# Inverse square roots in a decoder layer: a tuned seed, one tuned Newton step and one step of third order

## The chip, the cores and the metric

The kernel runs on one core of a Trainium2 chip. The metric is the device time of one execution in microseconds (us). The engines are TensorE (PE in the profile), VectorE (DVE), ScalarE (ACT), GpSimd (POOL) and SyncE (SP); they run side by side and wait for each other on semaphores.

## The reference

Input x is 8 sequences of 256 tokens with 256 features. One decoder layer is applied, in float32:

```
x = x + mamba(layernorm(x))            # in-projection, 4-tap convolution, chunked state scan, gated RMS norm, out-projection
x = x + cross(layernorm(x), context)   # 16 heads of 64, with an additive mask
x = x + ffn(layernorm(x))              # causal attention, 16 heads of 16, and 4 experts, top 2, both behind an RMS norm
# layernorm: (x - mean) / sqrt(var + 1e-5);  RMS norm: x * rsqrt(mean(x*x) + eps) * gain
```

Every norm needs one inverse square root for each token. A token is a row, so a group of 512 tokens has 4 values in each of the 128 partitions.

## The kernel before

The weights are loaded once and split into a high and a low part, so that three products of rounded operands give one product of float32 precision (`split_matmul`, L97 to L102, whose operations all carry the lines L100 to L102). Then four groups of 512 tokens go one after the other through three stages: `stage_mamba` (tiles a_), `stage_cross` (b_) and `stage_attention` (c_). Each stage is a block: all engines meet at its end. At the end `stage_experts` (e_) routes all 2048 tokens and runs 35 tiles of 128 slots through the experts. The order of the work on each engine is the order in which the code is written; nothing is scheduled by a program.

`inverse_root_of` takes values in one tile of a pair, uses the other as scratch, and writes their inverse square roots. `inverse_root` first adds the epsilon. All operations are on DVE and have 2 to 8 elements in each partition. `Chain.link` issues an operation and makes DVE wait until it has finished, `Chain.then` issues it without waiting for it. There are 25 calls:

- one in `load_weights` (through `normed`, tile w_rstd), for the first group,
- in each group one at the end of `stage_mamba` (L629, tile a_rs), in front of the scaling of the out-projection (L633). PE has by then filled two banks with out-projections and waits for L633 before it fills them again,
- one at the start of `stage_cross` (L942, b_rstd), while PE projects the context,
- one at the start of `stage_attention` (L1360, c_roots, 8 elements: two norms at once), which all PE work of the stage follows,
- one for the next group's first norm (L1424, through `normed`, c_rstn), while PE and ACT lay out the attention's operands,
- two at the end of `stage_attention` (L1454, c_rs, 2 elements each), one for each half of the group, in front of L1456.

Of the kernel before, what the change touches and what calls it, by code (L numbers as in the profile page):

```python
# [7 lines left out]
I32 = mybir.dt.int32  # L8
FR = mybir.dt.float32r
ALU = mybir.AluOpType  # L10
# [121 lines left out]
def inverse_root(dve, ch, out, var, eps, tmp):  # L132

    ch.link(dve.tensor_scalar(tmp[1], var, eps, None, ALU.add))
    inverse_root_of(dve, ch, out, tmp)


def inverse_root_of(dve, ch, out, tmp):

    hv, t = tmp  # L140
    ch.then(dve.tensor_scalar(hv, t, -0.5, None, ALU.mult))
    ch.link(dve.tensor_scalar(out.bitcast(I32), t.bitcast(I32), 1, None, ALU.logical_shift_right))
    ch.link(dve.tensor_scalar(out.bitcast(I32), out.bitcast(I32), -1.0, float(0x5F3759DF), ALU.mult, ALU.add))
    for _ in range(3):
        ch.link(dve.tensor_tensor(t, out, out, ALU.mult))
        ch.link(dve.tensor_tensor(t, t, hv, ALU.mult))
        ch.link(dve.scalar_tensor_tensor(out=out, in0=t, scalar=1.5, in1=out, op0=ALU.add, op1=ALU.mult))


def normed(dve, ch, out, x, st, mv, rstd, nt, ready):  # L150
# [892 lines left out]
def stage_attention(nc, ctx, g, I, W, K, XN, XG, RAW, rows_of, ps, s, weights_in, last):  # L1043

    weights, at_rows, at_out = rows_of
    with ExitStack() as own:
# [305 lines left out]
        def _(dve):  # L1352
# [5 lines left out]
            ch.link(dve.scalar_tensor_tensor(out=nt2[:, 1, 1], in0=nt2[:, 1, 0], scalar=RMS_EPS, in1=mv[:, :, 1],  # L1358
                                             op0=ALU.mult, op1=ALU.add))
            inverse_root_of(dve, ch, roots[:], (nt2[:, 0], nt2[:, 1]))  # L1360
            for t in range(GT):
                dve.tensor_scalar(xr[:, t, :], XG[:, t, :], mv[:, t, 0:1], scale[:, t:t + 1],
# [584 lines left out]
```

How the kernel before makes its waits and increments, by code:

```python
    def sync(self):  # L115
        if self.n:
            self.eng.wait_ge(self.sem, self.n)
# [43 lines left out]
def transposes_in(pe, src, ident, banks, tiles, ready, done):  # L161
    for t in range(GT):
        pe.wait_ge(ready, t + 1)
        for k in range(tiles):
            ins = pe.transpose(banks[k][:, t * P:(t + 1) * P], src[:, t, k * P:(k + 1) * P], ident)
            if t == GT - 1:
                ins.then_inc(done, 1)
# [30 lines left out]
        @block.sync  # L199
        def _(sp):
            sp.dma_start(XN[:], I["x"][0]).then_inc(s["x_in"], 16)
            for n, src in raws:
                sp.dma_start(raw[n][:], src).then_inc(loaded[n], 16)
            sp.wait_ge(s["x_in"], 16)
            sp.sem_inc(stored, 32)
# [1 line left out]
        @block.tensor  # L207
        def _(pe):
            pe.wait_ge(s["const_in"], 16)
            transposes_in(pe, xn, K["const"][:, C_ID:C_ID + P], ps, KD, s["x_normed"], s["x_turned"])
# [1 line left out]
        @block.scalar  # L212
        def _(act):
            act.dma_start(K["const"][:], I["const"][:, 0:C_N]).then_inc(s["const_in"], 16)
            for n in ("rope", "taps", "tapb", "nw", "g1", "g2", "dtb", "alog", "dpar"):
                act.dma_start(K[n][:], I[n]).then_inc(s["small_in"], 16)
            for i, (n, _) in enumerate(raws):
                if n == "wout":
                    act.wait_ge(s["wout_scaled"], 1)
                act.wait_ge(loaded[n], 16)
                act.activation(W[n][0][:], raw[n][:], ACT.Copy).then_inc(s["high_parts"], 1)
                if i == 1:
```

## Time and profile before

| | us |
|---|---|
| runs, median of 3 | 1502.42 (1502.37 to 1502.48) |
| profiled execution | 1502.61 |
| its span in the trace | 1500.7 |
| PE busy | 1225.5 (82%), 7994 matmuls |
| DVE busy | 1008.9 (67%), 3074 instructions |
| ACT busy | 638.3 (43%) |
| POOL busy | 265.4 (18%) |
| DMA, 16 engines | 80.32 MB, 54 GB/s |
| mean granted clock of TensorE | 0.90 of full speed |

The span is cut into engines' busy times. The clock of TensorE has two levels in this trace, 1.00 (2.4 GHz) and 0.50 (1.2 GHz); a stretch's mean between the two says that it held some of both. A wait of an engine that is not on the path to the end costs nothing, so the busy shares say where work is, not what a shorter operation is worth. For that one reads at each place who waits for whom.

### The profile page before, as it was taken

The numbers are of one execution on the slowest core, as the hardware profiler recorded it, in microseconds if no ns is written. First come the engines' busy times: TensorE is split into PE (matmuls) and PEld (weight loads), VectorE is DVE, ScalarE is ACT, GpSimd is POOL, SyncE is SP. The second block draws the span as 40 slices with busy tenths as digits, with TensorE's granted clock in tenths as the row PEclk, the third lists the DMA queues.
The fourth block names the chain that finished last, engine by engine and source line by source line (L and its number), as shares of the span: only waits on it lengthen the run. The fifth ranks groups of instructions, "written<-read, shape, count | busy, mean of one in ns | idle before, by whom it ended". The sixth has DMA issues, their size and how long they took to land. (4 is left out here: it accounts for less than half of the span.)

```text
span 1500.7 us, 24288 instructions
## 1 busy us (share of the span) xinstructions
PE 1225.5 (82%) x7994; PEld 1086.0 (72%) x7994; DVE 1008.9 (67%) x3074; ACT 638.3 (43%) x1370; POOL 265.4 (18%) x199
## 2 busy tenths in 40 slices
PE   1679987968799697779996968799787149999997
PEld 1467986946689696567996946689687148888886
DVE  6875766668477666785766668567667875555553
ACT  4325635733266175324644723256265403333331
POOL 2200003311000150100003301000141612333332
PEclk9889997988899888789997987899889559999999
DMA  6005510010164001004510010064330001222221
GB/s 231 1 1 123 136 38 1 2 56 1 42 145 96 15 1 42 15 1 113 134 36 15 1 57 1 22 154 106 143 125 10 21 14 25 40 36 36 37 41 23
DMA packets 45256, 80.32 MB, mean 54 GB/s; under 512 B 8432, under 2 KB 18160, under 8 KB 44496
## 3 DMA queue, kind: packets, MB, share of 16 engines
q1 hardware_dynamic: 36976, 69.19, 17.1%
q0 software_dynamic: 6720, 9.18, 3.8%
q8 instruction: 69, 1.13, 0.3%
q10 hardware_dynamic: 1440, 0.39, 0.1%
q14 instruction: 51, 0.42, 0.1%
HBM read 28.01 MB, written 8.78 MB: 25 GB/s over the span
## 5 line engine op out<-in xcount | busy, mean ns | idle before, releaser
L921 ACT ACTIVATE b_pp<-b_pp,b_nm 128x256 f32<-128x256 f32 x256 | 116.0, 501 | 86.9 <-DVE b_nm L959 86.0
L800 PEld LDWEIGHTS bank<-b_va,b_pt 128*128 128x128 f32 x1024 | 127.6, 191 | 4.0
L800 PE MATMUL bank<-b_va,b_pt 128*128 128x65 f32 x1024 | 128.5, 269 | 0.0
L1187 PE MATMUL bank<-c_kv,c_qv 128*128 128x128 f32 (+1 forms) x512 | 95.5, 316 | 7.3 <-ACT c_kv L1302 7.3
L1209 PE MATMUL bank<-c_v,c_pt 128*128 128x68 f32 x768 | 101.1, 268 | 0.1
L1145 POOL TENSOR_SCALAR c_qv<-c_rot,const 128x512 fp32r<-128x512 f32 x56 | 86.8, 1567 | 77.9 <-ACT c_rot L1298 77.9
L1209 PEld LDWEIGHTS bank<-c_v,c_pt 128*128 128x128 f32 x768 | 97.9, 192 | 1.7 <-DVE c_pt L1409 0.7
L959 DVE CUSTOM_DVE_ANT_0 b_pp<-bank,mask 128x256 f32<-128x256 f32 x256 | 97.0, 418 | 0.0
L100 PE MATMUL bank<-e_up_low,e_xh 128*128 x210 | 89.7, 427 | 1.8 <-DVE e_xl L178 1.8
L1401 DVE CUSTOM_DVE_ANT_0 c_pp<-bank,const 128x128 f32<-128x128 f32 (+1 forms) x256 | 80.2, 351 | 10.0 <-PE bank L1187 10.0
L1568 POOL DMA_INDIRECT out<-e_ys,e_ids x35 | 55.5, 1586 | 164.2 <-DVE e_ys L1803 160.4
L102 PE MATMUL bank<-e_up_high,e_xh 128*128 x210 | 84.3, 401 | 0.0
L1128 POOL MEMSET c_v<- 128x16 f32 x4 | 0.5, 126 | 473.0 <-POOLq L643 473.0
L787 PE MATMUL bank<-const,b_pp 128*128 128x128 f32 x512 | 77.7, 274 | 7.8 <-ACT b_pp L921 7.7
L101 PE MATMUL bank<-e_up_high,e_xl 128*128 x210 | 83.6, 398 | 0.0
L1672 ACT ACTIVATE e_th<-bank 128x512 f32<-128x512 f32 x35 | 21.0, 601 | 146.5 <-PE bank L102 146.5
L1786 DVE SCALAR_TENSOR_TENSOR e_th<-e_th,bank 128x512 f32<-128x512 f32 x70 | 38.8, 554 | 65.7 <-ACT e_th L1672 57.1
L773 PE MATMUL bank<-k_low_twice,b_qst 128*128 128x256 f32 x256 | 76.0, 321 | 7.1 <-DMA b_qst<-b_ql 7.1
L1187 PEld LDWEIGHTS bank<-c_kv,c_qv 128*128 128x128 f32 x512 | 73.3, 209 | 10.2 <-ACT c_kv L1302 10.2
L178 DVE SCALAR_TENSOR_TENSOR b_ql<-bank,b_qst 64x512 fp32r<-64x512 f32 x64 | 44.0, 688 | 52.4 <-ACT b_qst L892 30.9
L515 DVE SCALAR_TENSOR_TENSOR a_cv<-bank,taps,a_cv 128x510 f32<-128x510 f32 (+2 forms) x72 | 53.7, 746 | 37.3 <-ACT a_cv L461 35.6
L332 POOL TENSOR_TENSOR a_av<-a_a,const 128x1024 f32<-128x1024 f32 x16 | 30.2, 1896 | 244.5 <-DVE a_a L549 159.8
(368 smaller groups left out, 3631.2 us busy)
## 6 DMA issues: line engine op xcount, KB each, us to landing
b_kst<-b_kh SPq DMA_DIRECT2D x128, 128.0 KB, 2.3
k_low_twice<-b_kl SPq DMA_DIRECT2D x128, 128.0 KB, 2.4
b_qst<-b_ql SPq DMA_DIRECT2D x64, 128.0 KB, 2.3
raw_up<-in_w SPq DMA_DIRECT2D x4, 768.0 KB, 10.3
raw_down<-in_w SPq DMA_DIRECT2D x4, 768.0 KB, 12.1
XN<-in_x SPq DMA_DIRECT2D x5, 512.0 KB, 3.4
context<-in_ctxT SPq DMA_DIRECT2D x4, 512.0 KB, 4.7
mask<-in_mask SPq DMA_DIRECT2D x4, 512.0 KB, 5.6
```

What stands on the lines that cost most here:

```text
L100: pe.matmul(out, ah, bl, start=start, stop=False)
L101: pe.matmul(out, al, bh, start=False, stop=False)
L102: return pe.matmul(out, ah, bh, start=False, stop=stop)
L773: pe.matmul(out, qst[:, j % 2, hp, tokens(b, qt)], klst[j % 2][:, hp, b * S:(b + 1) * S], start=True, stop=False)
L787: ins = pe.transpose(T2[n % 2][:, kt * S + qt * P:kt * S + (qt + 1) * P], pp[:, n % 3, qt, kt * P:(kt + 1) * P], ident)
L800: ins = pe.matmul(O2[u % 2][:, at:at + VW], pt[:, n % 2, kt * S + qt * P:kt * S + (qt + 1) * P], va[:, b * QT + kt, 2 * j + hp, :], start= ...
L921: act.activation(pp[:, n % 3, qt, :], pp[:, n % 3, qt, :], ACT.Exp, bias=nm[:, n % 4, qt:qt + 1], scale=-1.0).then_inc(s["probs_exp"], 1)
L959: dve.tensor_tensor_reduce(out=pp[:, n % 3, qt, :], in0=S3[n % 3][:, qt * S:(qt + 1) * S], in1=mask[:, b * QT + qt, :], scale=-1.0, scalar ...
L1145: pool.tensor_scalar(qv[:, m % 2, r, :], qb, rows(r), None, ALU.mult).then_inc(s["q_masked"], 1)
L1187: ins = pe.matmul(SB[n % 3][:, qt * P:qt * P + w], qv[:, m % 2, r, at:at + P], kv[:, m % 2, part, b * S:b * S + w], start=part == 0, stop= ...
L1209: ins = pe.matmul(OB[u % 2][:, at:at + AKV * AVW], pt[:, n % 4, i * P:(i + 1) * P], v[:, b * QT + kt].rearrange("p a b -> p (a b)"), start ...
L1401: dve.tensor_tensor_reduce(out=pp[:, n % 4, w], in0=SB[n % 3][:, w], in1=causal[:, (QT - 1 - qt) * P:QT * P], scale=-AD ** -0.5, scalar=3e ...
```

## The change

`inverse_root_of` is rewritten. Before: an operation that scales the input, an integer shift and an integer subtraction for the seed, and three Newton steps of three operations, twelve in all. After: the seed in one operation (the value's bits times -0.5 plus a constant), a Newton step of three operations with tuned constants and a sign that is put right later, and a step of third order in five operations, of which one (the scaling of `out`) is issued without waiting for it: nine in all. Each call has three DVE operations fewer, 75 over the kernel. Nothing else in the code differs.

```
 def inverse_root_of(dve, ch, out, tmp):
-    hv, t = tmp
-    ch.then(dve.tensor_scalar(hv, t, -0.5, None, ALU.mult))
-    ch.link(dve.tensor_scalar(out.bitcast(I32), t.bitcast(I32), 1, None, ALU.logical_shift_right))
-    ch.link(dve.tensor_scalar(out.bitcast(I32), out.bitcast(I32), -1.0, float(0x5F3759DF), ALU.mult, ALU.add))
-    for _ in range(3):
-        ch.link(dve.tensor_tensor(t, out, out, ALU.mult))
-        ch.link(dve.tensor_tensor(t, t, hv, ALU.mult))
-        ch.link(dve.scalar_tensor_tensor(out=out, in0=t, scalar=1.5, in1=out, op0=ALU.add, op1=ALU.mult))
+    q, x = tmp
+    ch.link(dve.tensor_scalar(out.bitcast(I32), x.bitcast(I32), -0.5, float(0x5F1FFFF9), ALU.mult, ALU.add))
+    ch.link(dve.tensor_tensor(q, out, out, ALU.mult))
+    ch.link(dve.tensor_tensor(q, q, x, ALU.mult))
+    ch.link(dve.scalar_tensor_tensor(out=out, in0=q, scalar=-ROOT_A, in1=out, op0=ALU.add, op1=ALU.mult))
+    ch.link(dve.tensor_tensor(q, out, out, ALU.mult))
+    ch.then(dve.tensor_scalar(out, out, -0.375 * ROOT_B ** 5, None, ALU.mult))
+    ch.link(dve.tensor_tensor(q, q, x, ALU.mult))
+    ch.link(dve.scalar_tensor_tensor(out=q, in0=q, scalar=-10 / (3 * ROOT_B ** 2), in1=q, op0=ALU.add, op1=ALU.mult))
+    ch.link(dve.scalar_tensor_tensor(out=out, in0=q, scalar=5 / ROOT_B ** 4, in1=out, op0=ALU.add, op1=ALU.mult))
```

with `ROOT_B = 0.703952253` and `ROOT_A = 2.38924456`. Six lines are added above, so lines behind L147 are numbered 6 higher in the changed kernel.

This is DVE's order at the end of the mamba stage before (a_nt is the pair of scratch tiles, a_rs the result, L633 the scaled out-projection):

```order
L134 TENSOR_SCALAR a_nt<-a_ss 128x4
L141 TENSOR_SCALAR a_nt<-a_nt 128x4
L142 TENSOR_SCALAR a_rs<-a_nt 128x4
L143 TENSOR_SCALAR a_rs<-a_rs 128x4
L145 TENSOR_TENSOR a_nt<-a_rs 128x4
L146 TENSOR_TENSOR a_nt<-a_nt 128x4
L147 SCALAR_TENSOR_TENSOR a_rs<-a_nt,a_rs 128x4
...
L633 SCALAR_TENSOR_TENSOR XG<-bank,a_rs,XN 128x256
```

The three lines from L145 stand three times there. The same place in the changed kernel:

```order
L134 TENSOR_SCALAR a_nt<-a_ss 128x4
L145 TENSOR_SCALAR a_rs<-a_nt 128x4
L146 TENSOR_TENSOR a_nt<-a_rs 128x4
L147 TENSOR_TENSOR a_nt<-a_nt 128x4
L148 SCALAR_TENSOR_TENSOR a_rs<-a_nt,a_rs 128x4
L149 TENSOR_TENSOR a_nt<-a_rs 128x4
L150 TENSOR_SCALAR a_rs<-a_rs 128x4
L151 TENSOR_TENSOR a_nt<-a_nt 128x4
L152 SCALAR_TENSOR_TENSOR a_nt<-a_nt 128x4
L153 SCALAR_TENSOR_TENSOR a_rs<-a_nt,a_rs 128x4
L639 SCALAR_TENSOR_TENSOR XG<-bank,a_rs,XN 128x256
```

Between the epsilon and the scaling stand nine operations where twelve stood. No operation of another engine moves.

## Rows read from the trace of the kernel before

**Rows 1.** Timeline of DVE at the first group's mamba norm: start us, us, engine, line

```profile
94.53 0.17 DVE L141 TENSOR_SCALAR a_nt<-a_nt 128x4 f32<-128x4 f32 x1
94.61 0.16 DVE L142 TENSOR_SCALAR a_rs<-a_nt 128x4 int32<-128x4 int32 x1
...
96.78 0.48 DVE L633 SCALAR_TENSOR_TENSOR XG<-bank,a_rs,XN 128x256 f32<-128x256 f32 x1
```

**Rows 2.** Timeline of DVE at the attention stage's first norm and its last but one

```profile
222.78 0.17 DVE L141 TENSOR_SCALAR c_nt<-c_nt 128x8 f32<-128x8 f32 x1
...
225.07 1.38 DVE L1362 TENSOR_SCALAR c_xr<-XG,moments,c_roots 128x256 f32<-128x256 f32 x4
...
302.72 0.17 DVE L141 TENSOR_SCALAR c_nt<-c_nt 128x2 f32<-128x2 f32 x1
...
304.95 0.62 DVE L1456 TENSOR_SCALAR c_xr<-c_ln,c_rs 128x256 f32<-128x256 f32 x2
```

**Rows 3.** Timeline of PE behind these norms: in brackets idle before, and its releaser

```profile
97.41 0.55 PE L100 MATMUL bank<-wout_low,a_yh 128*128 128x256 f32 x1 [2.94 <-DVE XG L633]
...
225.54 0.69 PE L166 MATMUL bank<-const,c_xr 128*128 128x128 f32 x2 [5.55 <-DVE c_xr L1362]
...
305.63 0.55 PE L1220 MATMUL bank<-const,c_xr 128*128 128x128 f32 x3 [1.28 <-DVE c_xr L1456]
```

**Rows 4.** Timeline of DVE behind the load's and the cross stage's norm

```profile
18.26 4.46 DVE L260 TENSOR_TENSOR wv_low<-raw_wv,wv_high 128x2048 fp32r<-128x2048 f32 x1 [0.87 <-ACT wv_high L221]
...
111.16 0.69 DVE L950 COPY b_va<-bank 128x512 f32<-128x512 f32 x1 [1.55 <-PE bank L102]
```

**Rows 5.** Stretches: length, busy us of PE, PEld, DVE, ACT, POOL, then PEclk

```profile
107.30:110.60 3.30, 3.30 (x9) 2.56 (x8) 2.13 (x9) 0.60 (x1) 0.00 (x0) 0.50 0.00 0
315.50:318.88 3.38, 3.38 (x10) 2.17 (x9) 0.00 (x0) 0.67 (x2) 0.00 (x0) 0.50 0.94 326
318.88:322.30 3.42, 3.42 (x17) 2.66 (x17) 2.55 (x6) 1.82 (x3) 0.00 (x0) 1.00 0.04 16
336.00:342.70 6.70, 5.71 (x30) 5.07 (x30) 4.78 (x8) 3.64 (x7) 0.00 (x0) 0.75 0.00 0
598.80:602.19 3.39, 3.39 (x11) 2.24 (x10) 0.00 (x0) 0.98 (x2) 0.00 (x0) 0.50 0.88 324
602.19:605.60 3.41, 3.41 (x16) 2.71 (x16) 2.85 (x7) 1.81 (x4) 0.00 (x0) 1.00 0.00 0
1237.10:1243.80 6.70, 6.33 (x22) 4.66 (x21) 2.64 (x6) 1.50 (x4) 0.00 (x0) 0.75 0.00 0
```

**Rows 6.** Timeline of PE where its work begins again in three of these stretches

```profile
313.48 0.58 PE L100 MATMUL bank<-ul,win_high 128*8 128x512 f32 x1 [2.11 <-PEq L1046]
...
336.13 0.80 PE L100 MATMUL bank<-ul,win_high 128*128 128x512 f32 x1 [2.35 <-DVE a_cv L515]
...
1235.17 0.79 PE L100 MATMUL bank<-e_up_low,e_xh 128*128 x1 [1.45 <-DVE e_xl L178]
```

**Rows 7.** Timeline, two places of the mamba stage in the second and the third group

```profile
347.63 1.19 PE L401 MATMUL bank<-a_av,const 128*128 128x512 f32 x1 [0.71 <-DVE a_zg L564]
...
376.77 0.17 DVE L134 TENSOR_SCALAR a_nt<-a_ss 128x4 f32<-128x4 f32 x1
...
630.62 1.19 PE L401 MATMUL bank<-a_av,const 128*128 128x512 f32 x1 [0.71 <-DVE a_zg L564]
...
659.91 0.17 DVE L134 TENSOR_SCALAR a_nt<-a_ss 128x4 f32<-128x4 f32 x1
```

**Rows 8.** Timeline of DVE, two places of the attention stage in both groups

```profile
530.17 0.29 DVE L1401 CUSTOM_DVE_ANT_0 c_pp<-bank,const 128x128 f32<-128x128 f32 x1 [2.04 <-PE bank L1187]
...
583.13 0.42 DVE L1444 TENSOR_TENSOR c_ln<-c_ln,bank 128x256 f32<-128x256 f32 x1 [0.32 <-PE bank L102]
...
813.01 0.29 DVE L1401 CUSTOM_DVE_ANT_0 c_pp<-bank,const 128x128 f32<-128x128 f32 x1 [1.98 <-PE bank L1187]
...
866.19 0.42 DVE L1444 TENSOR_TENSOR c_ln<-c_ln,bank 128x256 f32<-128x256 f32 x1 [0.32 <-PE bank L102]
```

More of the change, by code:

```diff
@@ L135, in inverse_root @@
     inverse_root_of(dve, ch, out, tmp)
+ROOT_B = 0.703952253
+ROOT_A = 2.38924456
 def inverse_root_of(dve, ch, out, tmp):
-    hv, t = tmp
-    ch.then(dve.tensor_scalar(hv, t, -0.5, None, ALU.mult))
-    ch.link(dve.tensor_scalar(out.bitcast(I32), t.bitcast(I32), 1, None, ALU.logical_shift_right))
-    ch.link(dve.tensor_scalar(out.bitcast(I32), out.bitcast(I32), -1.0, float(0x5F3759DF), ALU.mult, ALU.add))
-    for _ in range(3):
-        ch.link(dve.tensor_tensor(t, out, out, ALU.mult))
-        ch.link(dve.tensor_tensor(t, t, hv, ALU.mult))
-        ch.link(dve.scalar_tensor_tensor(out=out, in0=t, scalar=1.5, in1=out, op0=ALU.add, op1=ALU.mult))
+    q, x = tmp
[8 more added lines that the diff above has]
+    ch.link(dve.scalar_tensor_tensor(out=out, in0=q, scalar=5 / ROOT_B ** 4, in1=out, op0=ALU.add, op1=ALU.mult))
 def normed(dve, ch, out, x, st, mv, rstd, nt, ready):
```

## The prediction

> **What bounds the kernel now.** I read the busy shares first: PE 82%, DVE 67%, so neither is the bound throughout, and a shorter DVE chain is worth something only where others wait for it. Next the timeline at each of the seven kinds of call, one by one, asking who starts right behind the chain; last the granted clock by stretches, because the page's row of clock digits is under 9 in some slices, and these slices repeat from group to group.
>
> At three kinds of place the chain is what everybody waits for. Behind the mamba norm PE has been idle 2.94 us when L633 lets it go on; behind the attention stage's first norm 5.55 us; behind the first of its two last norms 1.28 us [rows 3]. The second of the last two follows the first through DVE's own order (add, square, norm), and the stage's end follows it. At the other three kinds nobody waits. In the load, the wv split that DVE comes to later waits 0.87 us for ACT, which waits for weights. In the cross stage DVE has its norm done and then idles 1.55 us for PE [rows 4]. The next group's norm ends in an idle DVE too: 2.04 us until the scores come [rows 8].
>
> **The change part by part.** The chain before runs from L141 at 94.53 to L633 at 96.78, 2.25 us [rows 1]. L141 isn't waited for and costs 0.08 (94.53 to 94.61); the other eleven operations take 96.78 - 94.61 = 2.17, 0.197 each, start to start. The chain after has eight operations that are waited for and one that is not: 8 x 0.197 + 0.08 = 1.66. Saved: 0.59. With 8 elements the chain is 225.07 - 222.78 = 2.29, with 2 elements 304.95 - 302.72 = 2.23 [rows 2]; the same count gives 0.61 and 0.58. All kinds of operation in the new chain stand in the old one, so I take no other duration. If the unwaited operation cost a full slot, the saving would be 0.47; if it cost nothing, 0.67.
>
> On the path in each group: 0.59 + 0.61 + 2 x 0.58 = 2.36. Over four groups 9.4 us. The thirteen other calls I cost at nothing: four cross norms (cover 1.55), four of the next group (cover 2.04) and the one of the load (cover: ACT and the weights). I don't need their covers for more than 0.59, and they aren't used up: what stands behind them moves earlier by less than the chain. The bound on the load's call is 0 to 0.6. No wait is added, no DMA moves.
>
> **What the clock makes of it.** That 9.4 would be the answer if PE's clock didn't change under way. It does. In the second group the clock is at 0.50 (1.2 GHz) up to 318.88 and at 1.00 (2.4 GHz) behind it; in the third it is at 0.50 up to 602.19 [rows 5]. The two rises are 283.31 apart, although the work itself had by then moved: L401 starts 282.99 after its twin, 0.32 early against the rises, but L134, behind another low stretch in between, 283.14 after, 0.17 early [rows 7]. In the attention stage the same: 282.84, that is 0.47 early, going into the low stretch, and 283.06, 0.25 early, behind it [rows 8]. So the rises sit at times of their own, and where PE is the bound on both sides of one, what arrives d earlier leaves only d/2 earlier: the extra time before the rise is spent at half rate. I apply this half three times in a group: in the mamba stage, at the start of the cross stage (PE is without a gap at 0.50 from 107.30 to 110.60 [rows 5]), and in the attention stage. At the fronts of stages, where DVE is the bound, d passes in full.
>
> Group 1: nothing before the mamba norm. Then 0.59 saved; DVE waits for PE again at the last of the out-projections that follow, and part of them runs at the low clock, so that I keep 0.40 of it (between a half, 0.3, and all, 0.59); half in the cross stage, 0.20; + 0.61 = 0.81; half, 0.40; + 1.16 = 1.56 at the end of the group.
>
> If all rises stayed where they are, that would go on as d/8 + 1.6 and end near 1.8: locked. But they will not all stay. Before the rise at 318.88 PE had been without a gap since 313.48 [rows 6], 5.4 us. Other rises come after less: PE starts at 336.13, and the stretch from 336.00 to 342.70 has a mean of 0.75, so half of it is low and the rise is near 339.35, 3.2 us behind the start. With a start 1.56 earlier, at 311.92, I expect the rise one step earlier, and the low part of 3.35 us just read is that step: 318.88 goes to about 315.5, 3.5 us behind the start. I take the step as 3.4. What PE did at half rate in the 5.4 us is then done in 3.6 us at half rate and the rest, 1.8 us of half-rate work, in 0.9: at 316.4 in place of 318.9, d = 2.5, and DVE's convolutions follow with all of it. Against rises that all come 3.4 early this is 0.9 behind, which the next halving makes 0.5. If this rise didn't move, I expect the later one of the mamba stage to do so, since PE would then reach L401 1.56 earlier and be past its gap of 0.71 [rows 7]; either way the second group leaves its mamba stage 3.4 - 0.5 = 2.9 early. Then + 0.59 = 3.5, excess over a step 0.1; cross 0; + 0.61, halved, 0.3; + 1.16 = 1.5. From there each group repeats itself: one step, with an excess of 1.5 at its end. After four groups: 3 x 3.4 + 1.5 = 11.7.
>
> In the experts the routing before the first tile shifts as a whole. The first tile's projections start at 1235.17 [rows 6] and the clock rises half way through 1237.10 to 1243.80, near 1240.45 [rows 5], 5.3 us later. With an excess of 1.5 it is as in the second group: the rise comes one step sooner against the start. The low part shrinks from 5.3 to 3.4, and half of 1.9, 0.95, is gained. Behind it PE bounds every tile and nothing is lost. Sum: 11.7 + 0.95 = 12.6 (without that last step the excess is halved, and the sum is 10.9).
>
> The profiled execution took 1502.61 and gives 1490.0; it is 0.19 above the median of the runs, so against the median 1489.8. That is my forecast.
>
> The Trainium skill, "TensorE: Matmul & The Clock Gate", section "What's actually happening", says that where the clock rises differs from run to run and that one shouldn't fit to it. By that rule the steps average out and the gain is the plain 9.4. The times here speak against it: three runs lie within 0.11 us of each other, and a whole step would show.
>
> **The rivals.**
> A. Plain sum: the steps come at other places than I walked, and on average d passes in full. 9.4 saved, 1493.0. For it: my walk hangs on two margins (0.4 at the second group's rise, 0.2 at the experts'). Against: the halvings are measured.
> B. Locked: no rise moves. 1.8 at the end of the groups, halved in the experts: 0.9 to 1.8 saved, 1500.6 to 1501.5. For it: the groups repeat at 283.31 as if nothing else could be. Against: 1.56 is much more than the 0.3 that the groups drifted.
> C. Slower: the earlier arrival puts idle time together so that the clock falls once more in PE's gapless work. The place would be the start of the scores in the attention stage, where PE starts and stops. A low stretch of 3.4 costs 1.7, one of 10.2 (three steps) 5.1. It decides from two extra long ones in each group: 8 x 1.7 = 13.6 against 9.4, 4.2 slower, 1506.6. Against: PE's idle times get shorter with this change, not longer (2.94, 5.55 and 1.28 all shrink).
> D. The change doesn't do what it says: DVE's operations with a multiply and an add on integers, or the chain's last steps, cost a slot more each, and 0.2 and not 0.59 is saved: plain sum 3.2, 1499.2.
>
> **How the numbers follow.** Forecast with the experts' step 0.42, without it (10.9 saved, 1491.5) 0.2, A 0.2, B 0.06, C 0.02, D 0.04; 0.06 for more than forecast, a further step of 3.4 somewhere (cost 1.7), 1488.1. The range takes in the forecast, the case without the step, A with its 0.47 for a chain (7.5 saved would be 1494.9, a corner of A) in part, and the further step: 1488.0 to 1493.8. About 0.2% (3.0 us) is what a measurement of this kernel can tell from no change. Faster by more than that: all but B, C and half of D, 0.91; within: 0.07; slower: 0.02.
>
> **What would show it.** Each chain 1.65 to 1.70 long in place of 2.25. L633's waiter on PE idle about 2.4. The rises at the start of the groups no longer 283.31 apart but one step less, about 279.9, and the groups with them; the first group still ending only about 1.56 early. The experts' first rise 3.4 behind their first projection. If the groups are 281 apart with rises at uneven distances, A is right; if the rises stay at 283.31, B. I would be wrong altogether if the attention stage showed a low stretch that it hasn't now.

## The result: 12.1 us faster

| | before | changed |
|---|---|---|
| runs, median | 1502.45 us (1502.09 to 1504.98, 6 runs) | 1490.33 us (1489.40 to 1491.48, 6 runs) |
| ratio, 95% interval | | 0.9915 (0.9902 to 0.9928) |
| profiled execution | 1502.61 us | 1490.08 us |
| its span | 1500.7 us | 1488.2 us |
| DVE busy | 1008.9 us, 3074 instructions | 995.1 us, 2999 instructions |
| PE busy | 1225.5 us | 1221.8 us |

The forecast was 1489.8. The 12.1 us are 0.8% of the time. Sixteen chains on the path lose about 0.6 us each, 9.4 us in sum. Where the other 2.7 us come from is the subject of what follows.

The chain itself first. DVE's timeline at the first group's mamba norm in the changed kernel (start us, duration us, engine, line); it answers to [rows 1]:

```profile
94.67 0.17 DVE L145 TENSOR_SCALAR a_rs<-a_nt 128x4 int32<-128x4 int32 x1
94.88 0.16 DVE L146 TENSOR_TENSOR a_nt<-a_rs 128x4 f32<-128x4 f32 x1
...
95.66 0.17 DVE L150 TENSOR_SCALAR a_rs<-a_rs 128x4 f32<-128x4 f32 x1
95.74 0.15 DVE L151 TENSOR_TENSOR a_nt<-a_nt 128x4 f32<-128x4 f32 x1
...
96.32 0.48 DVE L639 SCALAR_TENSOR_TENSOR XG<-bank,a_rs,XN 128x256 f32<-128x256 f32 x1
```

From 94.67 to 96.32 it is 1.65 us, where 2.25 stood. L150 isn't waited for and costs 0.08 (95.66 to 95.74); every other step is about 0.2. With two elements the changed chain takes 304.04 - 302.40 = 1.64, by the first and the last of these rows:

```profile
302.40 0.17 DVE L145 TENSOR_SCALAR c_rs<-c_nt 128x2 int32<-128x2 int32 x1
...
304.04 0.61 DVE L1462 TENSOR_SCALAR c_xr<-c_ln,c_rs 128x256 f32<-128x256 f32 x2
```

PE's idle time behind the three norms, with the first operation after it (in brackets the idle time and who ended it); the rows answer to [rows 3]:

```profile
96.95 0.36 PE L100 MATMUL bank<-wout_low,a_yh 128*128 128x256 f32 x1 [2.33 <-DVE XG L639]
...
224.94 1.33 PE L172 MATMUL bank<-const,c_xr 128*128 128x128 f32 x5 [4.95 <-DVE c_xr L1368]
...
304.71 0.66 PE L1226 MATMUL bank<-const,c_xr 128*128 128x128 f32 x4 [0.67 <-DVE c_xr L1462]
```

2.94, 5.55 and 1.28 have become 2.33, 4.95 and 0.67: 0.61, 0.60 and 0.61 less. In the cross stage, where the chain was held to be hidden, the wait has grown instead. This DVE row answers to the second of [rows 4], which had 1.55:

```profile
111.17 0.69 DVE L956 COPY b_va<-bank 128x512 f32<-128x512 f32 x1 [2.42 <-PE bank L102]
```

Its start has not moved (111.16 before): DVE is done earlier and waits longer for PE. So far this is only the plain sum. The rest is seen where PE's work begins again: at the front of the second, third and fourth group, and at the experts' first tile. PE in the changed kernel:

```profile
311.72 0.59 PE L100 MATMUL bank<-ul,win_high 128*8 128x512 f32 x1 [2.11 <-PEq L1052]
...
591.63 0.58 PE L100 MATMUL bank<-ul,win_high 128*8 128x512 f32 x1 [2.12 <-PEq L1052]
...
871.12 0.58 PE L100 MATMUL bank<-ul,win_high 128*8 128x512 f32 x1 [2.15 <-PEq L1052]
...
1223.43 0.79 PE L100 MATMUL bank<-e_up_low,e_xh 128*128 x1 [1.45 <-DVE e_xl L184]
```

Two of the same places of the kernel before (the other two starts, 313.48 and 1235.17, are in [rows 6]):

```profile
596.48 0.59 PE L100 MATMUL bank<-ul,win_high 128*8 128x512 f32 x1 [2.12 <-PEq L1046]
...
879.54 0.58 PE L100 MATMUL bank<-ul,win_high 128*8 128x512 f32 x1 [2.11 <-PEq L1046]
```

| | before | changed | gained so far | forecast |
|---|---|---|---|---|
| front of group 2 | 313.48 | 311.72 | 1.76 | 1.56 |
| front of group 3 | 596.48 | 591.63 | 4.85 | 1.56 + 3.4 = 4.96 |
| front of group 4 | 879.54 | 871.12 | 8.42 | 8.36 |
| experts' first tile | 1235.17 | 1223.43 | 11.74 | 11.7 |
| span | 1500.7 | 1488.2 | 12.5 | 12.6 |

The gain comes in steps of 3.1, 3.6 and 3.3, more than the 2.36 that the chains of a group give. The granted clock around these fronts (columns: length, busy us of PE, PEld, DVE, ACT, POOL, then the granted clock, the DMA share and GB/s), against [rows 5]:

```profile
309.10:315.80 6.70, 4.59 (x13) 2.38 (x12) 1.91 (x5) 1.43 (x3) 0.00 (x0) 0.50 0.70 223
315.85:322.60 6.75, 6.75 (x31) 4.96 (x31) 5.00 (x10) 2.33 (x4) 0.00 (x0) 1.00 0.23 90
589.00:595.70 6.70, 4.58 (x13) 2.34 (x12) 1.91 (x5) 1.43 (x3) 0.00 (x0) 0.50 0.72 221
595.75:602.50 6.75, 6.75 (x31) 4.96 (x31) 5.00 (x10) 2.33 (x4) 0.00 (x0) 1.00 0.23 89
868.90:875.60 6.70, 4.55 (x12) 2.54 (x12) 1.67 (x5) 1.43 (x3) 0.00 (x0) 0.50 0.75 238
875.65:882.40 6.75, 6.75 (x31) 5.01 (x31) 5.23 (x10) 2.33 (x4) 0.00 (x0) 1.00 0.18 72
1220.00:1227.20 7.20, 4.43 (x11) 3.29 (x12) 0.79 (x3) 1.22 (x3) 2.48 (x3) 0.50 0.25 73
1227.25:1234.00 6.75, 6.37 (x33) 4.92 (x33) 3.91 (x9) 2.33 (x7) 0.00 (x0) 1.00 0.00 0
```

The rise of the clock stands near 315.8, 595.7 and 875.6, that is 279.9 apart where it was 283.3 (318.88 and 602.19 in [rows 5]). From PE's start to the rise PE now spends 4.1, 4.1 and 4.5 us at 0.50 (1.2 GHz), before 5.4, 5.7 and 5.95; in the experts 3.8 in place of 5.3. That is 5.8 us less at half rate, and what is done at full rate instead takes half, so an estimate of the gain is 2.9 us. With the plain sum of 9.4 it makes 12.3, and 12.5 were measured between the two spans. The sum is rough: it takes the 9.4 as passed on in full, while the first group passes on 1.76 of its 2.36, and it leaves out the low stretches further inside the groups.

### The profile page after: what moved, and what is told of

Read it like the earlier page. It is cut to its first block and busy times, and to the rows that moved or that the text cites. A ratio compares the mean times of both kernels' runs of the same rounds, so it can differ in the third digit from the quotient of the medians.

```text
span 1488.2 us, 24213 instructions
## 1 busy us (share of the span) xinstructions
PE 1221.8 (82%) x7994; PEld 1082.5 (73%) x7994; DVE 995.1 (67%) x2999; ACT 639.2 (43%) x1370; POOL 265.3 (18%) x199
## 5 line engine op out<-in xcount | busy, mean ns | idle before, releaser
L1193 PEld LDWEIGHTS bank<-c_kv,c_qv 128*128 128x128 f32 x512 | 73.3, 209 | 10.2 <-ACT c_kv L1308 10.2
L1318 ACT ACTIVATE c_pp<-c_pp,c_nm 128x128 f32<-128x128 f32 x128 | 51.5, 402 | 50.6 <-DVE c_nm L1407 50.5
## 6 DMA issues: line engine op xcount, KB each, us to landing
raw_up<-in_w SPq DMA_DIRECT2D x4, 768.0 KB, 10.1
raw_down<-in_w SPq DMA_DIRECT2D x4, 768.0 KB, 12.1
```

The source lines that it names most:

```text
L1193: ins = pe.matmul(SB[n % 3][:, qt * P:qt * P + w], qv[:, m % 2, r, at:at + P], kv[:, m % 2, part, b * S:b * S + w], start=part == 0, stop= ...
```

## The experiments

Each was measured beside the kernel before, whose median there was 1502.99 (first four below), 1503.82 (next four), 1504.98 and 1504.32 (the last two pairs). Where times of different comparisons are set side by side, these differences of up to 2.5 us have to be kept in mind. Every statement on the clock below comes from one profiled execution of each kernel.

| kernel | median, us | ratio to before, 95% interval |
|---|---|---|
| nine operations at c_rs only | 1492.77 (1492.08 to 1494.64) | 0.9932 (0.9918 to 0.9945) |
| nine at a_rs and c_roots only | 1497.27 (1496.10 to 1500.11) | 0.9963 (0.9949 to 0.9977) |
| ten everywhere | 1491.22 (1490.10 to 1492.73) | 0.9918 (0.9905 to 0.9932) |
| eleven everywhere | 1497.12 (1495.70 to 1498.39) | 0.9956 (0.9943 to 0.9970) |
| nine at the calls on the path | 1489.93 (1489.00 to 1491.10) | 0.9913 (0.9900 to 0.9926) |
| nine at the hidden calls | 1503.61 (1502.11 to 1506.14) | 1.0002 (0.9994 to 1.0011) |
| fifteen everywhere | 1507.64 (1505.63 to 1510.36) | 1.0027 (1.0015 to 1.0039) |
| changed, GpSimd's copy later | 1497.83 (1492.65 to 1498.84) | 0.9957 (0.9944 to 0.9971) |
| PE's waits filled, nine | 1451.56 (1450.18 to 1452.82) | 0.9647 (0.9634 to 0.9660) |
| PE's waits filled, twelve | 1463.33 (1461.15 to 1463.62) | 0.9719 (0.9706 to 0.9733) |
| filled further, nine | 1446.71 (1445.34 to 1456.77) | 0.9634 (0.9607 to 0.9661) |
| filled further, twelve | 1456.66 (1453.10 to 1461.96) | 0.9686 (0.9666 to 0.9706) |

### Which calls bring it: on the path, and hidden

The old function was kept beside the new one as `inverse_root_twelve`, and a call takes one or the other. In the first kernel the load's norm, the cross norm and the next group's norm have the old one; in the second the four calls of each group that are on the path have it instead.

```
-def inverse_root(dve, ch, out, var, eps, tmp):
+def inverse_root(dve, ch, out, var, eps, tmp, root=None):
     ch.link(dve.tensor_scalar(tmp[1], var, eps, None, ALU.add))
-    inverse_root_of(dve, ch, out, tmp)
+    (root or inverse_root_of)(dve, ch, out, tmp)
...
-            inverse_root(dve, ch, rstd[:], mv[:, :, 1], LN_EPS, (nt[:, 0], nt[:, 1]))
+            inverse_root(dve, ch, rstd[:], mv[:, :, 1], LN_EPS, (nt[:, 0], nt[:, 1]), inverse_root_twelve)
```

> Nine operations at the four calls of each group that the prediction puts on the path (mamba norm, attention's first norm, its two last norms), twelve at the load's, the cross stage's and the next group's norm. If those thirteen calls are hidden: the same as the changed kernel, 1490.3. If they count in part (0.59 each, 7.7 in all): up to 1498.

> The complement: nine operations at the load's, the cross stage's and the next group's norm (9 calls), twelve at the others. Hidden: 1502.9, as before. If they count: down to 1495.

Measured: 1489.93 with the calls on the path (the changed kernel has 1490.33), 1503.61 with the hidden ones (before: 1503.82, ratio 1.0002). The sixteen calls on the path bring everything; the other nine (the load's, four cross norms, four of the next group) bring nothing that can be measured. The prediction and the first expectation call them thirteen; the list has nine. No number of the prediction rests on it, but the 7.7 of the expectation does: nine calls of 0.59 are 5.3, and the upper end would have been 1495.6.

### How much of it: ten, eleven and fifteen operations

One, two or three dependent operations that multiply by one were put behind the chain in all 25 calls, in the changed kernel for ten and eleven, in the kernel before for fifteen.

```
     ch.link(dve.scalar_tensor_tensor(out=out, in0=q, scalar=5 / ROOT_B ** 4, in1=out, op0=ALU.add, op1=ALU.mult))
+    for _ in range(1):          # 2 in the second, 3 behind the twelve in the third
+        ch.link(dve.tensor_scalar(out, out, 1.0, None, ALU.mult))
```

> The changed kernel with one more dependent operation of 0.197 us in each chain (a multiplication by 1.0), ten in all: 1.58 of path saved in each group instead of 2.36. Steps: 1.03 is left at the end of the first group, at the edge of what moves the rise at the front of the second group; so either about 1491.3 (it moves) or about 1501.3 (it doesn't), nothing between. Plain sum: 6.3 saved, 1496.1.

> The changed kernel with two more dependent operations of 0.197 us in each chain, eleven in all: 0.8 of path saved in each group. Steps: 0.5 is left at the end of the first group, no rise moves, 0.3 to 0.6 saved in all, 1502.0, groups 283.3 apart. Plain sum: 3.2 saved, 1499.2.

> The kernel before with three more dependent operations (multiplications by 1.0) in each chain, fifteen in all: 2.36 us of path added in each group, as much as the change takes away. Steps: before, the groups are held at 283.31 by the clock's rises, and a later start by 0.6 at the mamba norm, 0.6 and 1.2 in the attention stage leaves (0.3 + 0.6) / 2 + 1.2 = 1.6 to 1.9 of delay that is not added up from group to group; 1.5 to 2.5 slower in all, 1505, groups still 283.3 apart. Plain sum: 9.4 slower, 1512.3, groups 285.6 apart.

Measured: 1490.3, 1491.2, 1497.1, 1502.5 and 1507.6 us with nine, ten, eleven, twelve and fifteen. By the plain sum each operation is worth 16 x 0.197 = 3.15 us. The steps are 0.9, 5.9 and 5.4, and three more cost 3.8 (against its own comparison's 1503.82) to 5.1 (against 1502.5), under the plain 9.4. Against the kernel before of each comparison, nine, ten and eleven save 12.1, 11.8 and 5.9. So the gain isn't proportional, and the steps are where I had put them only in part: of ten I had said that it either stays near nine (1491.3) or falls back to 1501.3, and it stayed. Eleven was expected to fall back to twelve, and came out between nine and twelve, nearer to its plain sum (1499.2) than to that. Fifteen was expected at 1505, with groups 283.3 apart. They are 283.3 apart, but the first group alone costs 5.7 in place of the 1.6 to 1.9 expected: PE begins the second group at 319.19, before at 313.48.

The clock shows why. With eleven operations the rise came 2.91, 5.98 and 3.06 us behind PE's start at the three fronts: in the second and fourth group it came a step earlier, in the third it did not. I had taken it that a rise comes no sooner than 3.2 us after PE's start.

### Which of the calls on the path

> The nine-operation chain stands only at the attention stage's two last norms (8 calls, 1.16 us of path in each group); all other calls have the twelve-operation chain. Steps (the gain is given out in steps of the clock's rises): the second group's matmuls begin 1.16 earlier, which I take to be enough for the rise at its front to come one step of 3.4 earlier in each of three groups; 3 x 3.4 + 1.0 = 11.2 saved, about 1491.2, groups 279.9 apart. Plain sum: 4 x 1.16 = 4.6 saved, 1497.8, groups about 282. The chains that nobody waits for are what counted: 1502.4.

> The nine-operation chain stands only at the mamba norm and at the attention stage's first norm (8 calls, 0.59 + 0.61 = 1.20 us of path in each group, as much as the two last norms have); all others have twelve. Steps: (0.40 / 2 + 0.61) / 2 = 0.4 is left at the end of the first group, too little for a rise to move; about 0.5 saved at the end of the groups and half of it behind the experts' rise, 1502.0, groups 283.3 apart. Plain sum: 4.8 saved, 1497.6, groups about 282.

The edit is the one above, with the new function at c_rs only (8 calls) and at a_rs and c_roots only (8 calls). Measured: 1492.77 and 1497.27. Half of the calls gives 10.2 us, of 12.1 in all, though their plain sum is 4.6; the other half, with a plain sum of 4.8, gives 5.7. Together 15.9, more than both at once: neither has a value of its own. The first result was expected and came 1.6 later than said. The second was not: by the steps no gain had been expected (1502.0). Its plain sum had said 1497.6, which is the time measured, with groups about 282 apart. They are 283.3 and 279.9 apart, so the mean is about that of the plain sum, but it is made up of whole steps. Its stretches around the fronts (columns as above):

```profile
309.10:315.80 6.70, 3.88 (x11) 1.93 (x12) 2.95 (x9) 0.84 (x3) 0.00 (x0) 0.50 0.55 168
315.90:322.50 6.60, 6.60 (x31) 4.93 (x30) 4.20 (x9) 2.81 (x5) 0.00 (x0) 1.00 0.38 140
589.00:595.70 6.70, 3.66 (x11) 1.71 (x12) 3.12 (x10) 0.84 (x2) 0.00 (x0) 0.50 0.52 158
595.80:599.10 3.30, 3.30 (x12) 2.23 (x11) 0.00 (x0) 1.21 (x2) 0.00 (x0) 0.50 0.83 306
599.20:602.50 3.30, 3.30 (x15) 2.67 (x15) 3.08 (x7) 1.60 (x4) 0.00 (x0) 1.00 0.00 0
872.30:879.00 6.70, 3.90 (x11) 1.95 (x12) 2.94 (x8) 0.87 (x3) 0.00 (x0) 0.50 0.54 164
879.10:885.80 6.70, 6.70 (x31) 5.04 (x30) 4.30 (x9) 2.79 (x5) 0.00 (x0) 1.00 0.39 144
```

and PE's starts in it:

```profile
313.04 0.58 PE L100 MATMUL bank<-ul,win_high 128*8 128x512 f32 x1 [2.11 <-PEq L1064]
...
593.16 0.59 PE L100 MATMUL bank<-ul,win_high 128*8 128x512 f32 x1 [2.12 <-PEq L1064]
...
876.22 0.59 PE L100 MATMUL bank<-ul,win_high 128*8 128x512 f32 x1 [2.11 <-PEq L1064]
```

The first front's start at 313.04 is only 0.44 earlier than before (313.48), and the rise is at 315.9, 2.8 us behind it, in place of 318.9. At the next front PE starts at 593.16 and the rise is at 599.2, 6.0 behind it; at the third 2.8 again. The 0.44 understates how much earlier PE comes to the rise, since the clock itself lies otherwise from one execution to the next: its first low stretch begins at 49.62 here and at 49.22 before. Counted from there PE's start is 0.84 earlier. The kernels side by side. The first column of times goes from PE's start at a front to the rise behind it, the second from the last front's rise to PE's start, the third from rise to rise:

| | start to rise, us, fronts of groups 2, 3, 4 | rise to start, us, groups 3, 4 | rise to rise, us | median, us |
|---|---|---|---|---|
| fifteen | 4.64, 4.05, 4.06 | 279.26, 279.24 | 283.3, 283.3 | 1507.6 |
| hidden calls only | 5.69, 5.50, 5.86 | 277.81, 277.44 | 283.3, 283.3 | 1503.6 |
| before | 5.40, 5.70, 5.95 | 277.60, 277.36 | 283.3, 283.3 | 1502.5 |
| a_rs and c_roots | 2.82, 6.00, 2.84 | 277.30, 277.06 | 283.3, 279.9 | 1497.3 |
| eleven | 2.91, 5.98, 3.06 | 277.33, 276.83 | 283.3, 279.9 | 1497.1 |
| c_rs only | 3.29, 3.44, 3.43 | 276.45, 276.46 | 279.9, 279.9 | 1492.8 |
| ten | 3.57, 3.23, 3.51 | 276.66, 276.38 | 279.9, 279.9 | 1491.2 |
| on the path | 4.30, 4.04, 4.06 | 275.86, 275.83 | 279.9, 279.9 | 1489.9 |
| changed | 4.1, 4.1, 4.5 | 275.8, 275.4 | 279.9, 279.9 | 1490.3 |

A rise is early where it stands 279.9 behind the one before, and not where the distance is 283.3. For the first front the distance is taken from the start of the first low stretch: 269.7 in the kernel before and with the hidden calls, 273.1 with fifteen operations, a step later, and 266.2, a step earlier, in the six others. So the early rises number none, two or three, and they sort the medians: 1502 to 1504, 1497, and 1490 to 1493; fifteen, with one rise a step late, has 1507.6. The distance from start to rise alone doesn't tell: fifteen has it as short as the fastest kernels.

The column from rise to start shows how close the kernel before stood to the next step. Fronts that PE began 277.06 us or less behind the last rise got theirs at 279.9, those that it began 277.30 or more behind at 283.3; before had 277.60 and 277.36. The walk had the three early rises of the changed kernel and none before, but its margin was wrong.

### The low stretch in the attention stage

The rival that ended slower had its place at the start of the scores. To get at it, GpSimd's copy of the repeated identity, which the kernel starts at the stage's front, was made to wait for the first norm.

```
             pool.memset(v[:, :, :, AD], 1.0).then_inc(s["ones_set"], 1)
+            pool.wait_ge(s["layer_norm_ready"], GT)
             pool.tensor_copy(repeat[:], identr.bitcast(F32).rearrange("p (a d) -> p a d", d=AD).unsqueeze(2)
```

> The changed kernel with GpSimd's fill of the repeat table (L1135, 1.05 us) put behind the stage's layer norm, where before it held up a DVE operation at the stage's start by 0.7 us (0.88 in place of 0.16). 0.7 us of path saved in each group, 2.8 by the plain sum, 1487.5. Steps: halved behind the attention stage's rise, 0.35 in each group and not added up; 0.3 to 0.6 faster, about 1489.9.

Measured: 1497.83, 7.5 us later than the changed kernel, where 1489.9 was expected; one of its six runs took 1492.65. Stretches at the scores' start, first of this kernel:

```profile
239.20:246.00 6.80, 2.45 (x10) 1.57 (x10) 4.94 (x23) 3.88 (x8) 2.11 (x4) 0.50 0.00 0
246.00:262.90 16.90, 16.89 (x78) 16.70 (x79) 5.91 (x33) 8.21 (x19) 8.39 (x6) 0.50 0.00 0
263.10:270.00 6.90, 6.90 (x66) 6.90 (x64) 4.29 (x23) 4.85 (x13) 1.00 (x1) 1.00 0.01 2
```

then of the changed kernel:

```profile
240.80:251.00 10.20, 7.73 (x36) 7.04 (x36) 4.98 (x26) 6.67 (x14) 4.39 (x3) 0.50 0.00 1
251.10:258.00 6.90, 6.90 (x61) 6.81 (x61) 4.25 (x26) 5.25 (x12) 4.82 (x4) 1.00 0.00 0
```

The low stretch of 10.2 us has become one of 23.9 (239.1 to 263.0), and again in the third group (802.3 to 826.2); in the second and fourth it is 13.6. PE was busy, as the profile models it, for 16.89 of the 16.90 us behind 246.00 and the clock stayed at 0.50 all through them. The rival's mechanism exists; the change didn't set it off, since the kernel before has a low stretch of the same length there, from about 240.3 to 250.6 by the means of these rows:

```profile
239.10:249.30 10.20, 5.98 (x27) 5.11 (x27) 7.15 (x37) 5.50 (x12) 4.19 (x5) 0.56 0.00 1
249.40:256.00 6.60, 6.60 (x55) 6.51 (x53) 3.09 (x16) 5.15 (x13) 5.47 (x4) 0.91 0.00 0
```

(5.7 of 10.2 us is 1.2 at 1.00 and 9.0 at 0.50; 0.91 of 6.6 leaves 1.2 at 0.50.) Why the clock stayed low through those 16.9 us stays open: the waits in front of it differ from the changed kernel's, and no run here varied them one at a time. The early rise at the three fronts (2.81, 4.53 and 2.98 us behind PE's start) was there in this kernel too; its loss is the attention stage's: the fronts of groups 2 and 4, behind the two long stretches, come 6.5 and 10.1 us later than in the changed kernel, the one between them 4.7.

### Taking the low clock out

If the extra 2.7 us are the clock's, the two kernels should be a plain sum apart once the clock doesn't fall. PE's waits were filled with matmuls that write a bank nobody reads at that time, 127 in a group, in the changed kernel and in the kernel before alike. The excerpt has notes in its comments that the code doesn't have.

```
+def fill(pe, bank, W, n):
+    w = W["awo"][0]
+    for _ in range(n):
+        pe.matmul(bank[:], w[:, 0, 0:P], w[:].rearrange("p k n -> p (k n)"), start=True, stop=True)
...
+            fill(pe, O2[0], W, 8)        # ahead of the cross stage's first wait
...
+            fill(pe, OB[0], W, 14)       # the attention stage's front, then 6, and 18 before the scores
...
+                fill(pe, BB, W, (4, 14)[hf])   # in front of c_rs's consumers
```

The others: in the mamba stage 11 and 8 in the convolution, 12 before the scan (behind a wait for the decay rates that was added there), 9 and 6 behind the out-projection's second and last tile; 4 at the cross stage's end; in the attention stage 6 before the first scores and 7 at the end.

> The changed kernel with PE's longer waits in each group filled by matmuls of N=512 whose results nobody reads (into banks that are free there), about 110 in a group, each wait filled to nine tenths at most, so that the clock doesn't fall in the groups. If the clock's low stretches are what sets the groups' lengths: the half-rate work in PE-bound places goes (2 us at a group's front, 1 to 2 behind the mamba norm, 2.4 at the cross stage's front, 3 to 5 in the attention stage), 24 to 36 us in all, 1455 to 1466. If they only went with waits that others set: no faster than 1490, or slower by the filling.

> The same filling in the kernel before (twelve operations in a chain). With no low stretches in the groups there are no steps, and the change is worth its plain sum: 9.4 us slower than the filled kernel with nine (8.5 to 10.5), groups 2.36 longer. If the steps aren't from the clock, the difference is 12, as without the filling.

Measured: 1451.56 and 1463.33, 11.8 apart. Both are far faster than their unfilled twins, by 39 us, the first by more than the 24 to 36 expected. But the difference was still 11.8, not 9.4, which by the expectation as written spoke for steps that aren't from the clock, unless the filling had left low stretches. The view of the first GpSimd copy of the attention stage, the same work once in each group, gives the distance from group to group: first and last start, divided by three. Filled with nine, then filled with twelve (count, shortest/median/longest ns, first and last start us):

```profile
L1153 POOL CAST c_repeat<-identr x4: 1037/1054/1057, 218.5 to 1027.5; 128x1024 fp32r<-128x1024 f32 x4
```

```profile
L1147 POOL CAST c_repeat<-identr x4: 1042/1056/1057, 220.3 to 1039.2; 128x1024 fp32r<-128x1024 f32 x4
```

(1027.5 - 218.5) / 3 = 269.7 and 273.0: 3.3 apart, still a step and not 2.36. The filling had left low stretches, and not the same ones. With nine there is one in each group, of 6.8 us (the first one at 64.1 to 71.0; here the second group's):

```profile
333.80:340.60 6.80, 5.90 (x15) 3.25 (x16) 3.79 (x9) 1.24 (x3) 0.50 (x1) 0.50 0.00 0
340.60:603.40 262.80, 246.47 (x1709) 218.33 (x1707) 188.34 (x636) 130.16 (x281) 34.83 (x29) 1.00 0.21 51
```

with twelve one more of 3.4 us in each group's attention stage (239.9, 513.0, 786.0, 1059.1); these two rows have that of the first group and the second group's other one:

```profile
239.90:243.30 3.40, 3.40 (x11) 2.60 (x10) 2.35 (x8) 2.42 (x5) 1.86 (x2) 0.50 0.02 5
338.90:345.70 6.80, 5.22 (x11) 2.68 (x12) 3.79 (x8) 1.29 (x3) 1.45 (x1) 0.50 0.00 0
```

So more was filled: 17 in place of 12 before the scan, 21 in place of 18 before the scores, three before each of two waits of the mamba and attention stages, and 26 before the experts' first tile.

```
-                    fill(pe, SM, W, 12)
+                    fill(pe, SM, W, 17)
...
+            pe.wait_ge(s["weights_high"], 1)
+            fill(pe, UC, W, 26, wh[0][:, 0, 0, 0:512].rearrange("p (k n) -> p k n", k=2))
```

> The filled kernel with nine operations still has one low stretch of 6.8 us in each group (first at 333.8), and its groups are 269.7 apart. Here the waits in front of it, and PE's wait before the first expert's tile, are filled too. No low stretch left between the first group and the routing: 1.5 us less in each group and 2 less in the experts, 1442 to 1447, and the groups free to take any length.

> The same with twelve operations. Steps from the clock: with no low stretch there are no steps, so the change is worth its plain sum: 9.4 us slower than with nine (8.9 to 9.9), every group 2.36 longer. If a low stretch stays in the groups, as in the two kernels filled less, the difference is a whole number of steps again (3.4 in a group, 11.8 measured there). If the steps have another cause: 11 to 12.

Measured: 1446.71 and 1456.66, 9.95 apart, where the plain sum says 9.4. The copies of the two kernels:

```profile
L1154 POOL CAST c_repeat<-identr x4: 1037/1056/1057, 218.7 to 1024.1; 128x1024 fp32r<-128x1024 f32 x4
```

```profile
L1148 POOL CAST c_repeat<-identr x4: 1038/1056/1057, 220.6 to 1032.9; 128x1024 fp32r<-128x1024 f32 x4
```

The two copies between them, first with nine, then with twelve operations:

```profile
488.02 1.04 POOL L1154 CAST c_repeat<-identr 128x1024 fp32r<-128x1024 f32 x1
...
756.31 1.06 POOL L1154 CAST c_repeat<-identr 128x1024 fp32r<-128x1024 f32 x1
```

```profile
491.07 1.04 POOL L1148 CAST c_repeat<-identr 128x1024 fp32r<-128x1024 f32 x1
...
761.94 1.05 POOL L1148 CAST c_repeat<-identr 128x1024 fp32r<-128x1024 f32 x1
```

The mean distances are 268.5 and 270.8, 2.3 from each other, as the chains' 2.36 say. One by one they are 269.3, 268.3 and 267.8 with nine, 270.4, 270.9 and 271.0 with twelve: 1.1, 2.6 and 3.2 apart, so only their mean has the plain sum. (With less filling the three differences were 3.5, 3.3 and 3.2.) Long stretches have the full clock, here two of the kernel with nine and one of that with twelve:

```profile
133.00:330.00 197.00, 190.30 (x1398) 174.25 (x1397) 139.48 (x527) 107.90 (x234) 31.38 (x26) 1.00 0.21 53
402.00:866.00 464.00, 441.84 (x3123) 395.41 (x3122) 330.60 (x1169) 238.63 (x516) 66.74 (x55) 1.00 0.21 52
```

```profile
336.00:875.00 539.00, 506.02 (x3470) 444.63 (x3469) 388.25 (x1320) 261.94 (x564) 70.89 (x58) 1.00 0.20 50
```

The expectation that no low stretch would be left failed: three of 3.4 us remain between the first group and the routing in each kernel, with nine at 330.4, 398.7 and 866.3, with twelve at 332.5, 875.3 and 943.5, and in front of the experts one of 58.0 and one of 6.8. In the first group the copy is 1.9 later with twelve, where the mamba norm accounts for 0.6; the low stretch in front of it (6.8 us from 125.6, and from 127.7) is 2.1 later. The runs of these two kernels spread more than the others (11.4 and 8.9 us), so the 9.95 would not settle between 9.4 and 11.8, and the two profiled executions are 10.7 apart. What the pair shows is that the even step of 3.2 to 3.5 in every group is gone when most of the low clock is; that the change is then worth exactly its plain sum is in keeping with it and not shown. This is also the fastest kernel here: 0.9634 of before (0.9607 to 0.9661), and 43.6 us under the changed one (57.6 and 12.1 us under the kernel before, each in its own comparison), with 590 matmuls more in it (8584 in place of 7994).

## Why the prediction was right, and where it was not

**The chain.** 2.25 to 1.66, 0.59 saved, was forecast by counting operations at 0.197 us; measured 1.65, and 0.61, 0.60 and 0.61 at the three waits of PE. Rival D, that the new operations cost more, is out by these rows. The count for 8 and 2 elements gives 0.60 and 0.59, where the prediction has 0.61 and 0.58; the sum changes by 0.01.

**On the path and hidden.** Sixteen calls on the path, nine beside it. The two complements gave 1489.93 and 1503.61: right, but for the thirteen.

**What the clock makes of it.** The steps (1.56, then 3.4 a group) were 1.76, 3.1, 3.6 and 3.3. The rises at the groups' fronts are 279.9 apart as forecast; rival B (283.3, 1501) and rival C (1506.6) are out. Rival A, the plain sum, is out for this pair of kernels (12.1 with an interval of 10.8 to 14.7 from the ratio, against 9.4). Where the clock is mostly kept up, its 9.4 agrees with what was measured (9.95, and 2.3 a group in the mean). Its sign, groups about 281 apart with rises at uneven distances, is what eleven operations and the a_rs and c_roots kernel show (283.3 and 279.9). That the forecast lies 0.5 us from the median is partly luck: the kernel before alone has medians from 1502.4 to 1505.0. Of the chances, those of a gain of more than 3.0 us add up to 0.90, with 0.08 for within, and not to 0.91 and 0.07.

**The first group.** Of the 0.6 of the mamba norm I let 0.20 reach the attention stage. Its first copy starts at 221.7 in both kernels, but the clock's low stretches up to there lie 0.39 later in the changed kernel's execution (the first from 49.61, before from 49.22). Counted from them the copy comes 0.4 earlier, so these two profiles can't tell 0.2 from nothing. The 0.60 of c_roots shrinks to 0.32 by the first c_rs (its epsilon operation starts at 302.20 in place of 302.52); that is near the half that was forecast, with the same reserve. The last consumer of c_rs starts 308.06 in place of 309.58, 1.52 earlier (forecast 1.56), and the next group's front 1.76. That 1.52 meets 1.56 so closely is in part luck.

**The step that was mis-sized: the gapless work ahead of a rise.** "Other rises come after less: ... 3.2 us behind the start", with a margin of 0.4 at the second group's rise. In these runs a rise stood as little as 2.8 us behind PE's start. The kernel before was nearer to the step than the walk had it, too: PE's starts at the fronts of groups 3 and 4, 277.60 and 277.36 behind the last rise, had to come only 0.3 to 0.5 us earlier. This is why eleven operations and the kernel with a_rs and c_roots alone, both expected to be at the level of before (1502.0), came out at 1497.1 and 1497.3, with the rise early in every other group. For the changed kernel itself the margin was wider than I thought: PE's 4.1 us against 2.8.

**The experts.** The rise was forecast 3.4 behind their first projection and a gain of 0.95; it stands 3.8 behind (1227.21), and 12.5 - 11.74 = 0.76 were gained. Half of the 1.5 us less at the low clock is 0.76 too.

**The page on the clock gate.** The Trainium skill, "TensorE: Matmul & The Clock Gate", section "What's actually happening", says that the place of a rise differs from run to run. I held against it that three runs lay within 0.11 us. That was weak: over all comparisons the kernel before ran from 1501.66 to 1506.31, and the first low stretch, in front of which the code differs by no more than the load's norm, begins at 49.2 in the profile of before, 49.6 in that of the changed kernel, and up to 51.4 in others. The trace agrees in part. The moments differ, by up to some 2 us. But the gain doesn't average out to the plain sum: the changed kernel's six runs stay within 2.1 us, where a kernel with one early rise less had 1497. By the page's rule the gain would be the plain 9.4; measured 12.1.

## What to carry to other kernels

In this kernel the granted clock falls and rises at the same places of a loop, and a saving on the path wasn't passed on as it is. Where a profile shows the same, read how long PE works at the low clock behind each start and how far each rise stands from the last, and be ready for a gain in steps: here one operation of sixteen chains was worth 0.9, 5.9 or 5.4 us, and a plain sum said 3.15. Before judging a small change by its time, fill PE's waits in both versions or compare several sizes of the change; and if PE's clock falls in waits, try to fill these waits first: here that was worth 43.6 us more on top of the change's 12.1. When two profiles are compared to a few tenths of a microsecond, compare first where the clock's first low stretch begins in each.

## What the runs showed of the hardware

GpSimd's copy held up a tiny operation of DVE. In the attention stage's front of the changed kernel:

```profile
221.88 0.88 DVE L1364 SCALAR_TENSOR_TENSOR c_nt<-c_nt,moments 128x4 f32<-128x4 f32 x1
```

while GpSimd copies from 221.69 for 1.05 us (its own view):

```profile
221.69 1.05 POOL L1135 CAST c_repeat<-identr 128x1024 fp32r<-128x1024 f32 x1
```

DVE's operation ends at 222.76, the copy at 222.74. With the copy moved behind the norm the same operation takes 0.16:

```profile
223.40 0.16 DVE L1377 SCALAR_TENSOR_TENSOR c_nt<-c_nt,moments 128x4 f32<-128x4 f32 x1
```

It is one operation in each group, 0.72 us in front of the chain; the kernel that saved it was slower all the same, for the low stretch told above.
